# Mixing two 512-token feed-forward slabs, instead of one, into the attention of a sandwich transformer layer

## The reference

```python
x = x + layernorm(attn(layernorm(x)))          # x: (2, 8192, 1024)
x = x + layernorm(ffn(layernorm(x)))
# attn: 16 heads of 64; sigmoid in place of softmax
w = sigmoid(q @ k.T * 64**-0.5);  w = w / (w.sum(-1) + 1e-6);  out = (w @ v) @ Wo.T
# ffn, ternary weights with a scale for each output column: 1024 -> 4096 -> 4096 -> 4096 -> 1024
h = silu(lin(x, w1)) * lin(x, w2)
h = gelu(lin(h, h1));  h = gelu(lin(h, h2));  out = lin(h, w3)
```

## Time and profile before

| | us |
|---|---|
| runs of the kernel | 7809.61 and 7891.58, median 7850.6 |
| the profiled execution, its own time | 7809.61 |
| its span on the slowest core (core 4) | 7808.0 |
| spans of the 8 cores | 7766.9 to 7808.0 |
| mean granted TensorE clock of the cores, share of full | 0.861 to 0.867 |
| PE busy in matmuls | 5678.4 (73% of the span) |
| ACT busy | 2657.4 (34%) |
| DVE busy | 817.5 (10%) |

### The profile page before, as it was taken

One profiled execution on the slowest core, in us unless ns is written; L12 is line 12 of the kernel. 1 busy time (PEld: TensorE's weight loads), 2 busy tenths in 40 slices (PEclk: granted clock), 3 DMA queues, 4 the chain that ended last, 5 costly groups with the idle time before them and its releaser, 6 DMA issues.

```text
span 7808.0 us, 67362 instructions; the slowest of 8 cores (7766.9 to 7808.0 us)
## 1 busy us (share of the span) xinstructions
PE 5678.4 (73%) x22418; PEld 2120.2 (27%) x22800; DVE 817.5 (10%) x727; ACT 2657.4 (34%) x2543; POOL 325.1 (4%) x574
## 2 busy tenths in 40 slices
PE   4735455477857678877878778766689999946886
PEld 1212112122212222222222222222234444412332
DVE  2221313000020000000000000024120000011001
ACT  2010101176727666666656666521200000010000
POOL 0000010000000000000000000000110000001000
PEclk6867777798978789988989889887899999979998
DMA  5344353411122222333332333332344444345665
GB/s 138 26 97 37 105 32 99 34 50 57 50 68 45 53 61 66 70 72 78 67 72 65 75 75 68 71 82 73 70 67 78 77 76 76 65 88 96 119 127 107
DMA packets 174502, 572.48 MB, mean 73 GB/s; under 512 B 20688, under 2 KB 86224, under 8 KB 133488
## 3 DMA queue, kind: packets, MB, share of 16 engines
q0 software_dynamic: 71776, 331.65, 27.5%
q1 hardware_dynamic: 102416, 236.50, 9.3%
HBM read 806.75 MB, written 50.72 MB: 110 GB/s over the span
## 4 chain that ended last, share of the span: by engine, by line
PE 53%; DMA 23%; ACT 10%; issue 9%; DVE 5%; SPq 0%; ACTq 0%; DVEq 0%; POOLq 0%
PE psG L917 20%; PE psS L576 9%; PE psO L615 9%; ACT wtil L588 8%; DMA V_sc<-vvo 8%; PE psF L872 4%; DMA wfb<-h 4%; DMA kbuf<-K_sc 4%; DMA wfb<-w 3%; PE psP L368 3%; PE psW L954 2%; DMA xs<-xT 2%; DMA y1f<-y_sc 1%; PE psA L719 1%; PE psP L394 1%
## 5 line engine op out<-in xcount | busy, mean ns | idle before, releaser
L588 ACT ACTIVATE wtil<-psS 128x1024 bf16<-128x1024 f32 (+1 forms) x1888 | 1955.5, 1093 | 970.8 <-PE psS L576 966.5
L917 PE MATMUL psG<-fb,wfb 128*128 128x512 bf16 x7957 | 1812.7, 383 | 112.5 <-DMA wfb<-h 88.5
L576 PE MATMUL psS<-qbuf,kbuf 64*128 64x512 bf16 x4096 | 1063.1, 415 | 729.6 <-ACT wtil L588 393.9
L615 PE MATMUL psO<-wtil,vbuf 128*65 128x512 bf16 x4096 | 1172.1, 416 | 12.0 <-ACT wtil L588 11.7
L917 PEld LDWEIGHTS psG<-fb,wfb 128*128 128x128 bf16 x8192 | 804.5, 99 | 1105.5 <-issue 174.7
L576 PEld LDWEIGHTS psS<-qbuf,kbuf 64*128 64x128 bf16 x4096 | 230.7, 95 | 1495.9 <-issue 1455.3
L615 PEld LDWEIGHTS psO<-wtil,vbuf 128*65 128x65 bf16 x4096 | 403.8, 117 | 736.2 <-issue 534.0
L419 PE MATMUL psV<-wvb,lnb 128*128 128x512 bf16 x1004 | 326.5, 496 | 346.1 <-DVE vvo L431 333.2
L872 PE MATMUL psF<-ln2tB,wfb 128*128 128x512 bf16 x1504 | 357.3, 387 | 220.6 <-DMA wfb<-w 191.4
L312 ACT ACTIVATE sq<-xs 128x2048 bf16<-128x2048 f32 x32 | 61.0, 1905 | 1016.2 <-DMA xs<-xT 1016.2
L636 DVE COPY rs_row<-psO 1x512 f32<-1x512 f32 x64 | 43.8, 685 | 2987.7 <-PE psO L615 2986.6
(11 more groups left out here) (107 smaller groups left out, 2212.9 us busy)
## 6 DMA issues: line engine op xcount, KB each, us to landing
wfb<-h POOLq DMA_DIRECT2D x192, 1024.0 KB, 8.4
vbuf<-V_sc SPq DMA_DIRECT2D x512, 130.0 KB, 2.6
xs<-xT SPq DMA_DIRECT2D x64, 1024.0 KB, 4.7
kbuf<-K_sc SPq DMA_DIRECT2D x32, 2048.0 KB, 8.3
wfb<-w POOLq DMA_DIRECT2D x192, 256.0 KB, 3.9
wfb<-w POOLq DMA_DIRECT2D x24, 1024.0 KB, 8.4
V_sc<-vvo POOLq DMA_DIRECT2D x64, 260.0 KB, 21.7
K_sc<-kvo POOLq DMA_DIRECT2D x32, 512.0 KB, 2.9
```

Source lines behind the costliest of these rows:

```text
L576: inst = e.matmul(psS[hh][:, j * QM:(j + 1) * QM], kbuf[kp][b:b + 64, (k0 + j) * 128:(k0 + j + 1) * 128], self.qbuf[b:b + 64, hp_ * T + q0 ...
L588: self.emit("act", lambda e, w=w, hh=hh, n=nk: e.activation(wtil[w][:, 0:n * QM], psS[hh][:, 0:n * QM], AF.Sigmoid, scale=ATT_SCALE), wait ...
L615: inst = e.matmul(psO[hh][:, :], vbuf[vslot][:, a_ * (DH + 1): a_ * (DH + 1) + DH + 1], wtil[w][:, j * QM:(j + 1) * QM], start=(k == 0), s ...
L917: inst = e.matmul(psF[p][:, tt * NT:(tt + 1) * NT], wfb[b][:, ic * 128:(ic + 1) * 128], s[:, ic * th + tt * NT: ic * th + (tt + 1) * NT], ...
```

## The change

It does four things. (1) `TW` becomes 1024: two query blocks go through attention alone, two through the mixed stage, and there are two slabs of 512 in the mixed stage, one after the other. (2) `ratio` is gone: one attention yield is drawn for each feed-forward unit. (3) The rest is one region of 1024 tokens, with one `phase2` and one `gen_phase3`. (4) In that last `gen_phase3` the squares and sums of the final layernorm are emitted within the w3 loop (`inline_stats`), right behind the copy of each output chunk; the two slabs of the mixed stage keep them behind the loop.

```diff
-        TW = 512 if T >= 1024 else T
+        TW = 512 if S <= 4096 else min(1024, T)
...
-            nmid = len(qms_b) * 8 * (S // 128 // 2 + 2)
-            nffn = (TW // 512) * 216
-            ratio = max(1, round(nmid / max(nffn, 1)))
...
                     if mid_alive:
-                        for _ in range(ratio):
-                            try:
-                                next(g_mid)
-                            except StopIteration:
-                                mid_alive = False
-                                break
+                        try:
+                            next(g_mid)
+                        except StopIteration:
+                            mid_alive = False
...
-        if regions:
+        if qms_b:
             scope_lnB = ExitStack()
-            ln2tBs = [scope_lnB.enter_context(
-                nc.sbuf_tensor(self.u("ln2tB"), [128, NCD * w], BF16)) for _, w in regions]
-            for (t0r, w), lt in zip(regions, ln2tBs):
-                self.phase2(t0r, w, lt)
+            ln2tB = scope_lnB.enter_context(nc.sbuf_tensor("ln2tB", [128, NCD * TW], BF16))
+            self.phase2(TW, TW, ln2tB)
             self.barrier()
             scope_o.close()
-            for (t0r, w), lt in zip(regions, ln2tBs):
-                for _ in self.gen_phase3(t0r, w, lt, t0r, w):
+            for t0f in range(TW, T, 1024):
+                for _ in self.gen_phase3(t0f, min(1024, T - t0f), ln2tB, TW, TW,
+                                         inline_stats=True):
                     pass
...
                             psW_free[par] = [("dve", self.c("dve"))]
+                            if inline_stats:
+                                fv = self.c("dve")
+                                self.emit("act", lambda e, o=oc, p=par, fbf=fbf, sq3=sq3: e.activation(
+                                    sq3[p][:], fbf[:, o * th:(o + 1) * th], AF.Square),
+                                    waits=[("dve", fv)] + sq_free[par], incs=[("act", 1)])
+                                actv = self.c("act")
...
+                                self.emit("pe", mk_stats, waits=[("act", actv), ("dve", fv)] + gw,
+                                          incs=[("pe", 1)])
+                                sq_free[par] = [("pe", self.c("pe"))]
                             yield
```

More of the change, by code:

```diff
@@ L242, in build @@
         else:
-            for _ in gen_ffn_a():
+            for _ in self.gen_phase3(0, 512 if T >= 512 else T, ln2tA, 0, TW,
+                                     inline_stats=True):
                 pass
@@ L970, in gen_phase3 @@
                             psW_free[par] = [("dve", self.c("dve"))]
-                            yield
[L973 to L1000, removed]
@@ new lines, in gen_phase3, with mk_stats @@
+                            yield
+                        if inline_stats:
+                            rows_done = self.ln_rows(ps3s, ps3q, th, self.rows["r"], self.rows["mr"])
+                    if not inline_stats:
+                        with ExitStack() as p3ctx:
+                            ps3s = p3ctx.enter_context(nc.psum_tensor(self.u("ps3s"), [1, th], F32))
+                            ps3q = p3ctx.enter_context(nc.psum_tensor(self.u("ps3q"), [1, th], F32))
+                            f_done = self.c("dve")
+                            sq_free = [[], []]
+                            for oc in range(NCD):
+                                par = oc % 2
+                                self.emit("act", lambda e, o=oc, p=par, fbf=fbf, sq3=sq3: e.activation(
+                                    sq3[p][:], fbf[:, o * th:(o + 1) * th], AF.Square),
+                                    waits=[("dve", f_done)] + sq_free[par], incs=[("act", 1)])
+                                actv = self.c("act")
+                                def mk_stats(e, o=oc, p=par, ps3s=ps3s, ps3q=ps3q, fbf=fbf, sq3=sq3):
+                                    for tt in range(NTT):
+                                        e.matmul(ps3s[0:1, tt * NT:(tt + 1) * NT], self.onesB[:],
+                                                 fbf[:, o * th + tt * NT: o * th + (tt + 1) * NT],
+                                                 start=(o == 0), stop=(o == NCD - 1))
+                                    for tt in range(NTT):
+                                        inst = e.matmul(ps3q[0:1, tt * NT:(tt + 1) * NT], self.onesB[:],
+                                                        sq3[p][:, tt * NT:(tt + 1) * NT],
+                                                        start=(o == 0), stop=(o == NCD - 1))
+                                    return inst
+                                gw = self.guard() if oc == 0 else []
+                                self.emit("pe", mk_stats, waits=[("act", actv)] + gw,
+                                          incs=[("pe", 1)])
+                                sq_free[par] = [("pe", self.c("pe"))]
+                                yield
+                            rows_done = self.ln_rows(ps3s, ps3q, th, self.rows["r"], self.rows["mr"])
```

24 lines of the change are left out of this document (17 added, 7 removed).

## The result

| | before | after |
|---|---|---|
| runs | median 7898.5 of 12, lowest 7809.6 | median 7245.4 of 14, lowest 7151.3 |
| ratio of the two | | 0.916, 95% interval 0.912 to 0.919 |
| span of the slowest core in the profile | 7808.0 (core 4) | 7200.7 (core 7) |
| mean granted TensorE clock of the cores | 0.861 to 0.867 | 0.867 to 0.875 |

The change makes the kernel 8.4% faster; 9.3% was forecast. The ratio is taken over undisturbed runs; the medians hold some in which the clock of one die was lower.

What follows compares the result with a forecast made beforehand. The mixed stage alternates between PE waiting for ACT and ACT for PE; the 512 slab alone is bound by its weight stream. +650.5 - 430 - 46 - 903 + 19 = -709.5 from 7809.6 gives 7100, plus 20: 7120 us, range 7020 to 7330.

Steps and rivals of the forecast that it cites:

- Rounds with 16 matmuls at 5.0: Mixed stage: 288 rounds (psG and psW of both slabs), paced by PE at 5.0 us, 1440 in all.
- Rival A: Mixed stage: stalls do not close, rounds cost today's less three tiles (7.0, 8.2, 3.7); +768, 7890 us; chance 0.06.
- w1 rounds at 5.5, bound by ACT: Mixed stage: 64 rounds with weights w1, ACT the bound, between 5.18 and 8.2 us, taken as 5.5: 352.
- rival D: Mixed stage and last slab: sums and head-pair waits at upper bounds, w1 rounds 7.9: 213 us more, 7330; chance 0.07.
- Change of head pair at 12: Mixed stage: 16 changes, PE waiting for the one kbuf's load, 12 us each, 192 in all; between 9 and 15.
- What each slab adds at its end: Mixed stage: broadcasts 22 us, second slab's first weights waiting for DVE 20; vbuf loads on SP some rounds ahead.
- Phase 2: The phase-2 stages: 414.9 us in three stages become 2 x 184.4 = 368.8, so 46 less.
- The 512 slab goes: End of the kernel: the 512-token slab run alone, bound by its weight stream, goes: 903.1 us less.
- Rival B: Mixed stage: the weight stream becomes the bound, 11.3 us a psG chunk, 200 us more, 7320; chance 0.08.
- Sums in the loop: Last slab's w3 loop: new PE waits in 8 chunks, 32 us, less 13 saved: +19, bounds -5 and +30.
- Rival C: Mixed stage: PE kept at half clock, the 288 rounds 9.7 us instead of 5.0: +1354, 8470; chance 0.02.
- The signs: Forecast wrong if the mixed stage lasts over 2750 us, or PE waits there for wfb, or for psS in psG rounds.

Runs made afterwards that it cites:

- e1: Kernel before with one attention yield per feed-forward unit, TW still 512: fastest 7515.6 us against 7892.8, ratio 0.952; mixed stage 2637 from 2948.
- e4: Changed kernel with Sigmoid in place of Silu and Gelu in the feed-forward part (another function): fastest 7045.5 us, mixed stage 2441 for 2565.
- e5: Kernel before, loading only half of each weight block's columns from the third load on: ratio 0.975; last feed-forward stages 2097 us for 2265.
- e6: Changed kernel, loading only half of each weight block's columns from the third load on: 0.909 of the kernel before; mixed stage 2537 us for 2565.
- e3: Changed kernel with the last slab's sums behind the w3 loop again: fastest 7144.0 us, last stage 1358.7 against 1385.2.
- e10: Kernel of e8 run again beside e11 on one chip: 0.893 of the kernel before, fastest 7077 us.
- e11: Kernel of e10 with the next head pair's first two value loads issued ahead of the row-sum stores: fastest 6973 us, mixed stage 2435.5.
- e8: Changed kernel with the next head pair's keys loaded early everywhere and the last sums behind the w3 loop: 0.885 of the kernel before, fastest 6940 us.

## Why the prediction was right, point by point

1. **Attention alone** (+650.5): 1293.7 for two blocks, 7 under.
2. **Rounds with 16 matmuls at 5.0**: 4.98 measured where nothing interferes. The reason given, that the ACT idle is filled rather than repeated, is what the rows show, and e1 gains 311 us by the alternation alone. Rival A (7.0 a round, 7890) falls with the same rows. The rounds of w3 were not so even: two with matmuls and the one that holds the copy took 4.98, 1.92 and 5.87 us, 12.8 for the forecast's 12.2.
3. **w1 rounds at 5.5, bound by ACT**: 5.25 apart, which is 1.28 + 0.69 + 1.28 + 1.94 and 0.06. e4 shows the bound: without the table loads the mixed stage loses 124 us, where 120 were expected for w1 and 140 in all. The rule that the prediction weighed, the Trainium skill's 2.66 us for a switch (ScalarE: Activation LUTs, What ACT_TABLE_LOAD costs), does not agree with this trace: a round with two switches at 2.66 would be 7.9, an estimate by that page's figure. By it the w1 term of rival D would have held; the measurement decides.
4. **Change of head pair at 12**: 13 of the 15 waits last 8.0 to 13.9 us, 10.2 in the mean, and work at the lower clock comes on top (the scores behind one took 1.24 us for 0.61, the unit behind them 4.65 for 3.62). Counted from the scores ahead of a change to the second scores behind it, the eight in the psG stretches cost 9.6 to 13.3 us more than three rounds of 4.98, 11 in the mean. So 12 was about right in size. The count was not: the sum has 16 changes and the start of the stage besides, and there are 15, which makes it 12 too high. The other two waits belong to the next point.
5. **What each slab adds at its end**: 2 broadcasts waited 13.6, as forecast. Here lies the largest miss within the mixed stage, in size and in understanding: the prediction said that `vbuf` loads queued on SP are some rounds ahead. They are not, and the key load is behind the same queue. The timeline of the changed kernel at the end of its first slab:

```profile
4229.52 0.34 SPq L1042 DMA_DIRECT2D out<-outb  x1
4229.95 0.87 SPq L550 DMA_DIRECT2D vbuf<-V_sc  x2
...
4234.47 1.89 PE L604 MATMUL psO<-wtil,vbuf 128*65 128x512 bf16 x4 [3.94 <-DMA vbuf<-V_sc]
...
4255.43 0.36 SPq L1042 DMA_DIRECT2D out<-outb  x1
4255.89 0.38 SPq L524 DMA_DIRECT2D kbuf<-K_sc  x1
...
4265.07 1.31 PE L565 MATMUL psS<-qbuf,kbuf 64*128 64x512 bf16 x4 [22.92 <-DMA kbuf<-K_sc]
```

   Each load is issued right behind a store of the output units, and those stores stood on SP for 68.0 us waiting for DVE between 4180 and 4290. PE had been free since 4242.2, but the keys were asked for at 4255.89. The same happens at the end of the second slab, so two of the 15 waits last 22.9 and 23.1 us instead of 10. Each stretch of the mixed stage, taken from its first feed-forward matmul to the first of the next kind, against the forecast's terms for it:

   | stretch | measured less forecast, us |
   |---|---|
   | ends of the two slabs and the tiles left over | +32 |
   | psG, both slabs | +18 |
   | w3, both slabs | +14 |
   | start of the stage | +2 |
   | w1 and w2, both slabs | -11 |
   | the 16th change of head pair, which there is not | -12 |

   The 44 is thus 66 too little less 23 too much. That they partly cancel is luck; in the psG stretches PE waited 7.7 us for weights, 6.9 for two Gelus and 3.6 for sigmoids, which is about their +18.
6. **Phase 2** (-46): 190.1 + 192.1, so -33 (on the median of the cores 186 and 188). 184.4 had been read on a phase 2 with another right behind it and no barrier between; whether that is the difference was not tested.
7. **The 512 slab goes** (-903.1): it does, and e5 shows that its weight stream, 8.54 us a load, was its bound. Rival B had the weights pace the mixed stage at 11.3 a chunk: PE waited 32.5 us for weights there, and e6 gains 28 from half of the bytes. It falls, but by less than the prediction thought: it had the weights asked for 11.3 us before use, and the rows show 9.6, against 9.0 to land. The kernel notes a buffer as free only behind the tile that follows the unit: of 60 issues in the window from 3400 to 4040, 58 waited for a `psO`.
8. **Sums in the loop** (+19): +26 by e3, within its bounds. The place was right, the size a quarter low, 5 of the 7 us by the three chunks at a lower granted clock.
9. **Rival C**, the lower clock: the mixed stage was granted 0.93, more than the 0.88 before. It falls.
10. **The signs**: the prediction called itself wrong if PE waits for `wfb` in the mixed stage. It did, 32.5 us in 26 waits. The sign had no size to it; these waits are 1.3% of the stage, too little to be rival B. The other two signs did not show: the stage lasted 2568 us, not over 2750, and in the psG rounds from 3381 to 4057 the scores waited for nothing but keys, four times.

The sum was 7100 for the profiled execution and 7201 was measured; the stages' differences are +44 (projections), -7 (attention alone), +13 (phases 2), +44 (mixed) and +8 (last slab). The first, nearly half, is in the projections, which the change does not touch.

## What to carry to other kernels

When two streams of work are interleaved by hand on an engine that is in order, the grain decides: put one unit of the one behind each piece of the other that its partner engine can work on meanwhile, and count a round as the longer of the engines' sums, not as today's mean less what is taken out. A long wait hides those that stand behind it on the same queue: before costing its removal, list what else is issued at that point and when it lands. And a reduction that needs a copy and a square of the chunk just computed does not belong directly behind that chunk on an in-order engine.

## What was not expected of the hardware

The projections, the same instructions in every kernel here, took 1517 us in the first profile (median of the cores), 1536 in the changed kernel's, and 1668 in those of e10 and e11, on the chip that gave 1537 in e8's. DVE's waits say where: `vvo` waits for its store.

```profile
DVE vvo L431 <- DMA V_sc<-vvo: 605.4, 56, 14.9
```

```profile
DVE vvo L421 <- DMA V_sc<-vvo: 718.0, 56, 17.5
```

The first is the kernel before, the second e11, 113 us more; the median landing of that store went from 21.7 to 25.5 us. The fastest run of the kernel before on that chip went from 7835 to 7948 between the same two sessions. Why it varies was not found. A difference of 100 us between two runs can come from this stage alone, so the stages must be compared one by one.
